# Attention scores, maxima and weighing moved to TensorE tiles of 64 rows by 32 columns, in a one-core Perceiver kernel

## The reference

```python
HEADS, D_MODEL = 16, 256;  D_K = 16
B, LQ, _ = q.shape          # 4, 256
LKV = k.shape[1]            # 4096
qh = (q @ Wq + bq).reshape(B, LQ, HEADS, D_K).transpose(0, 2, 1, 3)
kh = (k @ Wk + bk) ...      # 4 x 16 heads x 4096 x 16
vh = (v @ Wv + bv) ...
o  = softmax(qh @ kh.T / sqrt(D_K)) @ vh
x  = x + (o merged over the heads) @ Wo + bo
```

## Time and profile before

| what | us |
| --- | --- |
| median of three runs | 1431.7 (1428.06 to 1433.41) |
| the profiled execution | 1427.45 |
| its span in the trace | 1425.7 |
| TensorE matmuls busy | 1372.8 |
| VectorE busy | 1070.9 |
| ScalarE busy | 962.1 |

### The profile page before, as it was taken

The page is one execution under the profiler, slowest core; times in us unless marked ns, Lnnn a source line. Parts: engine busy times, 40 slices in busy tenths (PEclk is TensorE's granted clock), DMA queues, the critical chain, the costliest instruction groups (busy, mean ns, idle before and its releaser), DMA issues.

```text
span 1425.7 us, 32607 instructions
## 1 busy us (share of the span) xinstructions
PE 1372.8 (96%) x13186; PEld 757.5 (53%) x13186; DVE 1070.9 (75%) x2114; ACT 962.1 (67%) x1931; POOL 287.7 (20%) x321
## 2 busy tenths in 40 slices
PE   7799999999999999999999999998989999989998
PEld 4344444444444444444444545456547999856666
DVE  4787877778787778777778888835876768767757
ACT  5377777777777777777777666672896664448731
POOL 3353121222212222121222100000003100001210
PEclk9899999999999999999999999999999999999999
DMA  5865453335445335544424632002401320347000
GB/s 172 191 160 151 119 134 93 90 92 135 115 122 121 73 90 128 131 113 106 112 68 102 192 83 46 2 1 60 119 24 59 111 68 0 92 117 151 2 1 30
DMA packets 98790, 134.53 MB, mean 94 GB/s; under 512 B 11024, under 2 KB 74128, under 8 KB 92688
## 3 DMA queue, kind: packets, MB, share of 16 engines
q1 hardware_dynamic: 98640, 132.45, 36.8%
HBM read 94.15 MB, written 38.27 MB: 93 GB/s over the span
## 4 chain that ended last, share of the span: by engine, by line
PE 83%; DVE 7%; ACT 7%; issue 2%; DMA 1%; POOL 0%; SPq 0%; DVEq 0%; ACTq 0%; POOLq 0%
PE psum L546 19%; PE psum L566 18%; PE psum L527 7%; PE psum L592 4%; PE psum L632 4%; PE psum L2147 4%; PE psum L2121 3%; PE psum L1241 2%; PE psum L2866 2%; DVE peaks L693 1%; ACT probs L791 1%; ACT key_f L824 1%; PE psum L2876 1%; PE psum L275 1%; PE psum L1638 1%
## 5 line engine op out<-in xcount | busy, mean ns | idle before, releaser
L693 DVE TENSOR_REDUCE peaks<-psum 128x1 f32<-128x512 f32 x1024 | 654.6, 685 | 168.7 <-PE psum L527 157.1
L791 ACT ACTIVATE probs<-psum 128x512 f32<-128x512 f32 x1024 | 555.9, 595 | 126.8 <-PE psum L546 125.0
L546 PE MATMUL psum<-queriesT,keysT 64*128 64x256 bf16 (+1 forms) x4096 | 331.9, 272 | 11.0 <-ACT probs L791 9.8
L566 PE MATMUL psum<-probs,values 128*17 128x256 f32 x4096 | 320.5, 385 | 0.0
L546 PEld LDWEIGHTS psum<-queriesT,keysT 64*128 64x128 bf16 (+1 forms) x4096 | 171.9, 94 | 219.4 <-ACT probs L791 159.3
L527 PE MATMUL psum<-keysT,queriesT 64*128 64x512 bf16 x1024 | 210.2, 379 | 7.3 <-DVE peaks L693 4.0
L566 PEld LDWEIGHTS psum<-probs,values 128*17 128x17 f32 x4096 | 68.0, 95 | 160.4 <-issue 151.3
L927 POOL CAST key_parts<-key_f 128x512 bf16<-128x512 f32 x57 | 34.9, 612 | 516.0 <-ACT key_f L824 509.7
L592 PE MATMUL psum<-ctxT,wk 128*128 128x512 f32 x128 | 75.1, 670 | 2.2 <-DVE probs L736 0.9
L527 PEld LDWEIGHTS psum<-keysT,queriesT 64*128 64x128 bf16 x1024 | 59.8, 94 | 26.1 <-DVE peaks L693 17.5
L632 PE MATMUL psum<-wv,ctxT 128*128 128x256 f32 x256 | 72.0, 407 | 0.5 <-DVE probs L724 0.4
(11 more groups left out here) (315 smaller groups left out, 1647.7 us busy)
## 6 DMA issues: line engine op xcount, KB each, us to landing
keysT<-key_parts SPq DMA_DIRECT2D x186, 256.0 KB, 5.5
key_parts<-key_parts SPq DMA_DIRECT2D x90, 256.0 KB
ctx_nat<-in_ctx_dram SPq DMA_DIRECT2D x32, 256.0 KB, 3.2
ctx_in<-in_ctx_dram SPq DMA_DIRECT2D x24, 256.0 KB, 3.1
ctx_turned<-ctxT SPq DMA_DIRECT2D x24, 256.0 KB, 6.0
ctx_T<-ctx_turned SPq DMA_DIRECT2D x12, 512.0 KB, 3.9
qk_parts<-early_weights SPq DMA_DIRECT2D x24, 128.0 KB
q_parts<-q_parts SPq DMA_DIRECT2D x20, 128.0 KB
```

Of the source, the lines that this page charges most:

```text
L546: made = e.matmul(ps[j][:, e2 * S:(e2 + 1) * S], self.keysT[own, plane, i % RING, kt * P:(kt + 1) * P], self.queriesT[own, plane, u % 2, g ...
L566: made = e.matmul(k.bank(SUMS)[32 * quad:32 * quad + DH + 1, 0:S], self.values[b % 2][:, kt, g * GH + j, :], self.probs[:, (SLOTS * i + p) ...
L693: e.tensor_reduce(self.peaks[:, i % 2, j * QT + qt, c:c + 1], k.ps(("max", n)), AX.X, ALU.max).then_inc(*self.peaked.up(n))
L791: e.activation(self.probs[:, t % RINGP, 2 * j * S:(2 * j + 2) * S], k.ps(("scores", t, j)), ACT.Exp).then_inc(*self.exped.up((t, j)))
```

## The change

- Scores: each matmul of 64 rows by 128 columns is cut into four of 64 rows by 32 columns (STRIP), one after another over the four quarters of the columns. A slot's scores are now given head by head: the "early" head's first step (4 matmuls), and its other three steps (12) after half of a weighing; the "late" head's four steps after the maxima, two before and two after the second half of the weighing. Which head is early alternates from slot to slot (order).
- Maxima: each is cut into four strips too, strip by strip for both heads. Both banks are taken before the first of them.
- Weighing: each matmul over 128 rows becomes two over 64, on the row half that the early head's scores, then the late head's, leave free. The two halves add up in the same bank, and the second waits for the end of the first (a new semaphore, half_weighed).
- Slots with t mod 16 = 2 have no weighing, and the next slot has two (weighings).
- ScalarE takes the exponentials in the new order of the heads. What was counted in blocks of slots (BLOCK = 1) is counted in slots, with the same values.

```diff
-SCORES, SUMS, BLOCK = (0, 1, 2), 3, 1
+HALVES, SUMS, STRIP = 3, 3, P // 4
+def order(t):
+    return (0, 1) if t % 2 else (1, 0)
...
+            for col in range(0, P, STRIP):
+                for j in range(GH):
+                    own, q = slice(j * HALF, (j + 1) * HALF), qt * P + col
+                    made = e.matmul(ps[j][col:col + STRIP, :], self.queriesT[own, MAIN, u % 2, g, q:q + STRIP],
+                                    self.keysT[own, MAIN, i % RING, c * BANK:(c + 1) * BANK], start=True, stop=True)
+                    if col == P - STRIP:
+                        made.then_inc(*self.max_made[j].up(n + j))
+
+        def score(t, j, first, last):
+            i, p = divmod(t, SLOTS)
+            u, g = divmod(i, UNIT_GROUPS)
+            if first == 0:
+                banks.use((2 * t + order(t).index(j)) % HALVES, w, ("scores", t, j), (self.exped, (t, j)))
+            ps = k.ps(("scores", t, j))
+            for step in range(first, last):
+                e2, plane = divmod(step, 2)
+                kt, own = 2 * p + e2, slice(j * HALF, j * HALF + (TALL if plane == REST else HALF))
+                for col in range(0, P, STRIP):
+                    at = kt * P + col
+                    made = e.matmul(ps[col:col + STRIP, e2 * S:(e2 + 1) * S], self.keysT[own, plane, i % RING, at:at + STRIP],
+                                    self.queriesT[own, plane, u % 2, g, :], start=(plane == MAIN), stop=(plane == REST))
+            if last == 4:
+                made.then_inc(*self.scored[j].up((t, j)))
+
+        def weigh(v, half, begins, ends):
+            i, p = divmod(v, SLOTS)
+            b, g = divmod(i, NG)
+            own = slice(half * HALF, (half + 1) * HALF)
+            for e2 in range(2):
+                for j in range(GH):
+                    quad, at, kt = e2 * GH + j, 2 * j + e2, 2 * p + e2
+                    made = e.matmul(k.bank(SUMS)[32 * quad:32 * quad + DH + 1, 0:S],
+                                    self.values[b % 2][own, kt, g * GH + j, :],
+                                    self.probs[own, v % RINGP, at * S:(at + 1) * S],
+                                    start=(p == 0 and begins), stop=(p == SLOTS - 1 and ends))
+            if begins:
+                made.then_inc(*self.half_weighed.up(v))
+            else:
+                made.then_inc(*self.weighed.up(v))
...
+            early, late = order(t)
+            due = self.weighings(t)
+            scoring = 0 <= t < TOTAL
+            if scoring:
+                w.wait_ge(self.shiftT_kept, t // SLOTS)
+                w.wait_ge(self.ones_in, 0)
+                score(t, early, 0, 1)
+            for v in due:
+                i, p = divmod(v, SLOTS)
+                w.wait_ge(self.exped, (v, order(v)[1]))
+                w.wait_ge(self.v_kept, (i // NG, p))
+                w.wait_ge(self.ones_set, i // NG % 2)
+                if i:
+                    w.wait_ge(self.outT_kept, i - 1)
+                w.wait_ge(self.cleared, 0)
+                weigh(v, 1 - early, True, False)
+            if scoring:
+                score(t, early, 1, 4)
+                if not due:
+                    score(t, late, 0, 4)
+            for n in maxima[::GH]:
+                find_maxima(n, t)
+            if scoring and due:
+                score(t, late, 0, 2)
+            for v in due:
+                w.wait_ge(self.half_weighed, due[-1])
+                weigh(v, 1 - late, False, True)
+            if scoring and due:
+                score(t, late, 2, 4)
...
+    def weighings(self, t):
+        if t % SLOTS == 2 or not 3 <= t <= TOTAL + 1:
+            return ()
+        return (t - 3, t - 2) if t % SLOTS == 3 else (t - 2,)
...
-                for j in range(GH):
+                for j in order(t):
                     w.wait_ge(self.scored[j], (t, j))
```

More of the change, by code:

```diff
@@ L387, in __init__ @@
         self.peaked, self.exped = sig("peaked"), sig("exped")
-        self.weighed, self.outT_kept = sig("weighed"), sig("outT_kept")
+        self.weighed, self.half_weighed, self.outT_kept = sig("weighed"), sig("half_weighed"), sig("outT_kept")
         self.gathered, self.heads_scaled = sig("gathered"), sig("heads_scaled")
@@ L514, in misc, with find_maxima @@
             return banks.use(choice[turn % len(choice)], w, job, *let_go)
-        def find_max(n, now):
-            i, j, qt, c = self.max_at(n)
+        def find_maxima(n, now):
+            ps = {}
+            for j in range(GH):
+                job, let_go = ("max", n + j), (self.peaked, n + j)
+                ps[j] = banks.use(4 + (n + j) % 3, w, job, let_go) if now < -1 else misc(now, job, let_go)
+            i, _, qt, c = self.max_at(n)
             u, g = divmod(i, UNIT_GROUPS)
-            own = slice(j * HALF, (j + 1) * HALF)
-            job, let_go = ("max", n), (self.peaked, n)
-            ps = banks.use(4 + n % 3, w, job, let_go) if now < -1 else misc(now, job, let_go)
             w.wait_ge(self.rows_here[u % 2], u)
@@ L526, in find_max @@
                 w.wait_ge(self.pieces_here[c * self.PIECES // CH], 0)
-            e.matmul(ps, self.queriesT[own, MAIN, u % 2, g, qt * P:(qt + 1) * P],
-                     self.keysT[own, MAIN, i % RING, c * BANK:(c + 1) * BANK],
-                     start=True, stop=True).then_inc(*self.max_made[j].up(n))
+            for col in range(0, P, STRIP):
[5 more added lines that the diff above has]
+                        made.then_inc(*self.max_made[j].up(n + j))
@@ L531, in tensor @@
         for t in range(FIRST, TOTAL + 3):
             maxima = self.maxima(t)
[L533 to L536, removed]
-                w.wait_ge(self.ones_in, 0)
[L538 to L541, removed]
-                        for j in range(GH):
[L543 to L558, removed]
+            early, late = order(t)
+            due = self.weighings(t)
+            scoring = 0 <= t < TOTAL
@@ L780, in scalar @@
                 if t >= RINGP:
-                    w.wait_ge(self.weighed, (t - RINGP) // BLOCK)
+                    w.wait_ge(self.weighed, t - RINGP)
                 elif t == 0:
@@ L794, in scalar @@
                 i = t // SLOTS - 1
-                w.wait_ge(self.weighed, (t - BLOCK - 1) // BLOCK)
+                w.wait_ge(self.weighed, t - 2)
                 if i:
@@ L861, in scalar @@
                     if b >= 2:
-                        w.wait_ge(self.weighed, NG * SLOTS * (b - 1) // BLOCK - 1)
+                        w.wait_ge(self.weighed, NG * SLOTS * (b - 1) - 1)
                     elif b:
@@ L1083, in wait_first @@
         f = self.first
-        w.wait_ge(f.weighed, TOTAL // BLOCK - 1)
+        w.wait_ge(f.weighed, TOTAL - 1)
         w.wait_ge(f.outT_kept, GROUPS - 1)
@@ L1091, in wait_early @@
         f, u = self.first, B * KD - 1
-        w.wait_ge(f.weighed, TOTAL // B * (B - 1) // BLOCK - 1)
+        w.wait_ge(f.weighed, TOTAL // B * (B - 1) - 1)
         w.wait_ge(f.ctx_saved, (B - 1, CH - 1))
```

## The result

The changed kernel takes 1591.54 us (median of four runs, 1576.67 to 1592.15) where the kernel before takes 1430.06 (1428.06 to 1433.41): a ratio of 1.110 [1.103, 1.117]. Forecast were 1360 us and a range up to 1460. The profiled execution took 1591.96, 164.5 us more than before's 1427.45.

What follows compares the result with a forecast made beforehand. TensorE was taken as the bound, busy 96%. Gains of 2.9 us per 16 slots over 32 groups made 93 us; less 20 for near misses, 73 off 1427.5 gave 1355, forecast as 1360 us at the median, range 1325 to 1460.

Steps and rivals of the forecast that it cites:

- (e): TensorE's instructions: 18 to 56 matmuls a slot, each with its weight load, taken to cost 0, up to 10 us above.
- Rival three: TensorE can't take 56 matmuls and loads in 1.33 us; at 30 ns each, slots of 1.68 and 1545 us; chance 0.09.
- (b): Streaming in a plain slot: row halves run beside each other, 1.14 falls to 1.105 us, 0.4 us per 16 slots.
- Rival two: TensorE keeps program order, so score steps wait behind the weighing; plain slots 1.38 us, 1457 us in all; chance 0.16.
- the rule that the prediction quoted: From the Trainium skill: matmuls start and end strictly in program order, only weight loads are pulled ahead.
- (a): One tile shape for a slot's work saves 22 passages between shapes at 0.095 us: 2.1 us per 16 slots.
- (c): Slot 2 without weighing and slot 3 with two: some 2.63 us against 2.66, no gain, no loss.
- (d): Slot 0's wait for ScalarE's key block and shift copies gets covered: 0.86 us for two slots, 0.4 beyond other terms.
- the 93 of the sum: Gains of 2.1, 0.4 and 0.4, together 2.9 us per 16 slots, times 32 groups, before near misses.
- near misses: Small waits on VectorE and ScalarE, put at 20 us (0 to 56) and taken off the gain.
- (f): ScalarE's exponentials, 1.09 us a slot against TensorE's 1.105, stay hidden without margin; score banks free early enough.
- rival one: VectorE becomes the bound: plain slots fall only to 1.32 us, 35 us gained, 1393 or 1397 us; chance 0.16.

Runs made afterwards that it cites:

- half_columns_thin_reads: Changed kernel without score and maxima strips of columns 64 to 127, and key transfers cut to a sixteenth from the fourth group on: 1382.75 us.
- spread_one: Changed kernel with a group's six key transfers given one per slot over six slots instead of all in one slot: 1509.64 us.
- half_columns: Changed kernel with the strips of columns 64 to 127 of scores and maxima left out, 36 matmuls a slot for 56: 1431.35 us.
- tiles_64: Kernel before the change, with only scores and maxima cut to tiles of 64 by 64, 28 matmuls a slot: 1439.97 us.
- mixed_after_jobs: Changed form only in slots 0, 5 to 8, 14, 15 of each 16, others as before, weighing in every slot, key transfers spread: 1411.88 us.
- thin_reads: Changed kernel with key transfers cut to a sixteenth from the fourth group on: 1473.82 us.

## Why the prediction was wrong

**The step that failed is (e).** It counted 38 more matmuls a slot and 2.5 MB of instructions quite rightly (4.23 for 1.70 MB, 258 packets) and priced them: "I take 0", "with up to 10 us above". It set the bytes against what the DMA engines can carry, 0.5% of their time. The time of one block was the number to set: how long until the next is there (3.3 us from packet to packet at best, up to 8.6 behind a burst of keys), against how long one lasts (2.5 us). The measured price is 209 us: 1591.5 for the 1382.75 of half_columns_thin_reads, which has the change's order without the shortage. Nor did the sum have a term for the half clock that follows the stops.

**Rival three was the nearest, with another mechanism.** It would decide at 24 ns for a matmul and its load. In a short stretch less than that is enough. The starts of the maxima in plain slots of the changed kernel:
```profile
354.06 0.40 PE L536 MATMUL psum<-keysT,queriesT 64*32 64x512 bf16 x8
355.17 0.43 PE L536 MATMUL psum<-keysT,queriesT 64*32 64x512 bf16 x8
356.31 0.43 PE L536 MATMUL psum<-keysT,queriesT 64*32 64x512 bf16 x8
357.92 0.29 PE L553 MATMUL psum<-queriesT,keysT 64*32 64x256 bf16 x4 [0.69 <-issue]
```
1.11 us for 56 pairs is 20 ns each: the decoding holds. What doesn't hold is the supply, 26 ns a pair at best, and here too the slots end in a stop for instructions. Where it expected "starts at even distances", there are bursts at full speed and stops. Its 1545 us is the nearest of the forecasts to what was measured, and by luck, as its slot of 1.68 us isn't there (its own terms, 1427.5, 112 and the 4 beside the median, give 1544). The prediction's range left it out; no row of before could show the limit, as a block lasted 11 us there, but the bound from above was open and should have been in the range.

**Step (b) was right.** Forecast for a plain slot were 1.105 us (1.07 to 1.14); 1.11 to 1.14 it is, where instructions are there. The row halves do run beside each other:
```profile
600.68 0.29 PE L553 MATMUL psum<-queriesT,keysT 64*32 64x256 bf16 x4
...
600.70 0.41 PE L566 MATMUL psum<-probs,values 64*17 64x256 f32 x4
...
600.80 0.39 PE L553 MATMUL psum<-queriesT,keysT 34*32 34x256 bf16 x7
```
Rival two, the strict order, wanted step 1 of the scores after the weighing's second passes at 0.245 us; it starts 0.12 after step 0. So the trace speaks against the rule that the prediction quoted, as the earlier trace rows did. The earlier trace rows leave out a third row of the same view, which was less clear:
```profile
1049.89 1.64 PE L1638 MATMUL psum<-qT,kT 32*128 32x256 f32 x16
```
The test that the prediction set itself, plain slots under 1.25 us, was met and missed the matter: it asked for the length of a slot and not for the stops between slots.

**Steps (a), (c) and (d) in part.** half_columns_thin_reads shows what the order is worth without stops. Its stage:
```profile
L553 PE MATMUL psum<-queriesT,keysT x8192: 266/269/417, 67.4 to 915.8; 34*32 34x256 bf16 x101, 64*32 64x256 bf16 x99
```
That is 848.4 us for before's 895.6. By the starts of the slots in both traces (medians over the groups), a plain slot gains 0.21 us for 0.22 forecast. Slots with another job gain 0.02 to 0.06, not the 0.12 of step (a), and slot 15 nothing, so the price of a passage isn't one number. Slot 0 falls from 3.00 to 2.33: (d) was right in kind, 0.67 for 0.86 forecast. Slots 2 to 4 lose 0.55 us, 0.41 of them in slot 4; (c) took slots 2 and 3 to be even, and slot 4 had no term. A group so gains 1.8 us in the middle case and 1.5 on average, and not 2.9: 48 us in 32 groups for the 93 of the sum. Even without the shortage of instructions 1360 would have been 23 us too low, though inside the forecast's 1335 to 1390; the 20 us taken off for near misses hid part of the excess.

**Step (f) and rival one.** VectorE was hardly the bound: 4.8 us of waits of the maxima for it in 800, 7 with the other lines, where TensorE is fastest. As a price for such waits 20 us was too much.

**What stays open.** Stops and half clock can be told apart only in part. The changed kernel's stage is 209 us longer than that of half_columns_thin_reads; TensorE stands for 118 us more of it, and it has 150 us at half clock, worth at most 75. spread_one has 77 us more of idleness and 24 us at half clock for a stage that is 122 us longer, so the stops are the greater part; some 15 to 35 us are left over in either count. Nor was it tried why a block takes 1.1 us or more from landing to its first instruction, or whether it could be fetched sooner.

## What to carry to other kernels

When a change multiplies an engine's instructions, work out how long a block of 256 of them lasts in the densest stretch, whatever share of the DMA engines the instructions need. Here 2.5 us was too short; 3.9 us (half_columns) was enough only without the burst of keys, and 6.1 us (tiles_64) with it too. Short dense runs were bearable where the mean was 5.9 us (mixed_after_jobs). A stretch that runs dense must not stand beside a burst of large transfers; spread these over slots, or leave part of the slots in the form with few instructions. And a cost without a row that shows it needs its upper bound in the range, even where an average says that it is nothing.

## What the runs showed of the hardware

- One packet of 16 KB on the instruction queue for 256 TensorE instructions; in the changed kernel it lasts 0.9 to 1.7 us, the instructions run 1.2 us or more after its landing, and packets follow at 3.3 us or more in every run. With more than 297 records still to run before its own, no packet was fetched.
- The fetch was not let past data: behind 1.5 MB of keys a packet began 7.9 us after the one before, and TensorE stood for 4.0 us.
- After that stop of 4.0 us the granted clock was 0.50 (1.2 GHz) with TensorE at work again; in thin_reads, whose stops are shorter, the mean clock of the run is 0.983 against 0.944 in the changed kernel.
- A plain slot's 56 matmuls and 56 loads on tiles of 64 by 32 run in 1.11 us, 20 ns a pair.
